# Moving pieces of a decoder kernel's seam between attention and feed-forward rows, and one normalisation inside each row

## What is computed

```
x = LN(x + attn(x))     # 16 heads of 128, decayed linear attention, silu on q k v, rms norm, sigmoid gate, Wo
x = LN(x + wkv(x, ctx)) # per channel: running sums aa, bb over the tokens, y = (e1*aa + e2*v) / (e1*bb + e2)
x = LN(x + ffn(x))      # layer norm, ternary w_fc (2048x512), exact gelu, layer norm, ternary w_proj (512x2048)
```

## Time and profile before

| | |
|---|---|
| median of 3 runs | 1342.81 us (1342.69 to 1343.02) |
| the profiled execution | 1341.81 us, of which the span of the trace is 1340.0 us |
| PE busy | 1289.2 us, 96% of the span |
| DVE, ACT, POOL busy | 964.5 us (72%), 629.8 us (47%), 297.8 us (22%) |
| chain that ended last | PE 56%, ACT 7%, issue, DVE and POOL 2% each |
| mean granted TensorE clock | 0.993 |

### The profile page before, as it was taken

The page is one execution under the profiler, slowest core; times in us unless marked ns, Lnnn a source line. Parts: engine busy times, 40 slices in busy tenths (PEclk is TensorE's granted clock), DMA queues, the critical chain, the costliest instruction groups (busy, mean ns, idle before and its releaser), DMA issues.

```text
span 1340.0 us, 20153 instructions
## 1 busy us (share of the span) xinstructions
PE 1289.2 (96%) x7468; PEld 831.7 (62%) x7468; DVE 964.5 (72%) x1882; ACT 629.8 (47%) x1138; POOL 297.8 (22%) x213
## 2 busy tenths in 40 slices
PE   5899999999999999999999999999996999999997
PEld 3566666666666666666666666666664555555553
DVE  5875775696677767766776686677778688898763
ACT  3443343334334333433443334335364678888854
POOL 2112110111011111111111111111134665555530
PEclk9999999999999999999999999999998999999999
DMA  5100021121120111011111011010010011110000
GB/s 182 63 17 16 24 88 32 48 79 64 32 71 25 48 32 40 24 57 40 36 45 32 32 48 48 17 41 16 5 59 1 33 32 48 48 48 32 17 17 32
DMA packets 19103, 55.83 MB, mean 42 GB/s; under 512 B 2624, under 2 KB 2624, under 8 KB 18624
## 3 DMA queue, kind: packets, MB, share of 16 engines
q1 hardware_dynamic: 19008, 54.55, 12.3%
HBM read 50.35 MB, written 4.19 MB: 41 GB/s over the span
## 4 chain that ended last, share of the span: by engine, by line
PE 56%; ACT 7%; issue 2%; DVE 2%; POOL 2%; POOLq 0%; ACTq 0%; DVEq 0%
PE bank L399 7%; PE bank L400 7%; PE bank L401 7%; PE bank L613 3%; PE bank L614 3%; PE bank L471 3%; PE bank L473 3%; PE bank L472 3%; PE bank L414 2%; PE bank L416 2%; PE bank L415 2%; PE bank L639 2%; PE bank L638 2%; PE bank L623 1%; PE bank L442 1%
## 5 line engine op out<-in xcount | busy, mean ns | idle before, releaser
L399 PE MATMUL bank<-x_hi,w_hi 128*128 128x512 f16 x768 | 294.2, 383 | 5.2 <-DVE w_lo L1077 2.9
L1123 DVE TENSOR_TENSOR resid<-resid,bank 128x512 f32<-128x512 f32 x256 | 173.2, 685 | 174.3 <-PE bank L473 173.7
L400 PE MATMUL bank<-x_lo,w_hi 128*128 128x512 f16 x768 | 293.2, 382 | 0.0
L401 PE MATMUL bank<-x_hi,w_lo 128*128 128x512 f16 x768 | 293.1, 382 | 0.0
L1578 POOL TENSOR_TENSOR sq_sum<-sq_sum,o_sq 128x512 f32<-128x512 f32 x64 | 106.8, 1668 | 800.5 <-ACT o_sq L757 800.5
L757 ACT ACTIVATE o_sq<-bank 128x512 f32<-128x512 f32 x64 | 38.3, 598 | 291.4 <-DVE gated L1129 291.4
L414 PE MATMUL bank<-wv_hi,x_hi 128*128 128x256 f16 x512 | 139.6, 273 | 1.0 <-DVE x_lo L1138 0.5
L415 PE MATMUL bank<-wv_lo,x_hi 128*128 128x256 f16 x512 | 139.6, 273 | 0.0
L416 PE MATMUL bank<-wv_hi,x_lo 128*128 128x256 f16 x512 | 139.6, 273 | 0.0
L399 PEld LDWEIGHTS bank<-x_hi,w_hi 128*128 128x128 f16 x768 | 76.3, 99 | 91.4 <-issue 19.1
L401 PEld LDWEIGHTS bank<-x_hi,w_lo 128*128 128x128 f16 x768 | 75.6, 98 | 92.1 <-issue 2.7
(11 more groups left out here) (174 smaller groups left out, 2657.1 us busy)
## 6 DMA issues: line engine op xcount, KB each, us to landing
w_raw<-w_ffn SPq DMA_DIRECT2D x32, 512.0 KB, 3.6
raw_a<-w_heads SPq DMA_DIRECT2D x32, 256.0 KB, 3.9
raw<-w_heads SPq DMA_DIRECT2D x15, 512.0 KB, 3.6
raw<-w_heads SPq DMA_DIRECT2D x18, 256.0 KB, 3.9
x_in<-x_rows SPq DMA_DIRECT2D x8, 512.0 KB, 4.4
out<-y_out SPq DMA_DIRECT2D x8, 512.0 KB, 2.6
resid<-x_t SPq DMA_DIRECT2D x3, 1024.0 KB, 8.1
val<-ctx_t SPq DMA_DIRECT2D x6, 512.0 KB, 3.5
```

The source lines that it names most:

```text
L399: mm(bk[:, :], a, c, start=kt == 0, stop=False)
L400: mm(bk[:, :], a, d, start=False, stop=False)
L401: last = mm(bk[:, :], b, c, start=False, stop=kt == KT - 1)
L1123: tt(resid[:, 4 * g + t, :], resid[:, 4 * g + t, :], YB[t % 2][:, :], ALU.add).then_inc(y_added, 1)
```

## The change

In the last pair, unit 6: ACT's `exps1(1, 1)` and `exps2(1, 1)` move ahead of `square(61)` and the evacuation of G. DVE's `aa_states(0)` moves ahead of `split_probs(61)`, and `correct(0, 0)`, `correct(0, 1)` ahead of `gate(61)`; `input_sum(2)` leaves the unit. Unit 7: both halves of `split_x2(0)` and DVE's `bb_states(1)` move ahead of `square(62)` and `gate(62)`; `input_norm(2)` and `shift(NX, 2)` leave the unit.

Behind the last pair: `input_sum(2)` now stands behind `add_y(62, 3)` and ahead of `gate(63)`; `scale_columns` and `shift(NX, 2)` follow `gate(63)`, and `aa_states(1)` follows the last `add_y`. On POOL `miss(0)` goes ahead of `numerator(0)`, and `root(NX, 2)` from ahead of `second_root(0)` to behind `add_squares(62)`.

In every row with an `input_norm`, now row 0 too, it stands behind the second gelu instead of ahead of the first.

```diff
@@ ACT, unit of the last pair
+                if last_pair and t == 6:
+                    exps1(1, 1)
+                    exps2(1, 1)
                 if last_pair and t == 7:
                     second_norm(0, 0, SC)
+                    split_x2(0)
                 if lag1:
                     square(u - 1)
                 evacuate(u, t, G, first_unit)
...
-                if last_pair and t == 6:
-                    exps1(1, 1)
-                    exps2(1, 1)
                 if last_pair and t == 7:
-                    split_x2(0)
-                    input_norm(2)
                     exp_ln_tables()
                     invert(1)
@@ ACT, row
-                if second_row and not first:
-                    input_norm(b + 2)
                 act.wait_ge(scfc_ok, b + 1)
                 for f in range(4):
                     gelu(b, 0, f)
                     if first and f == 1:
                         square(UNITS - 1)
+                    if second_row and f == 1:
+                        input_norm(b + 2)
@@ DVE, unit of the last pair
+                if last_pair and t == 6:
+                    aa_states(0)
                 if lag1:
                     split_probs(u - 1)
                 split_q(u)
...
-                if last_pair and t == 6:
-                    aa_states(0)
...
                 after_unit(t)
+                if last_pair and t == 6:
+                    correct(0, 0)
+                    correct(0, 1)
+                if last_pair and t == 7:
+                    bb_states(1)
+                    split_x2(0)
                 if lag1:
                     gate(u - 1)
...
-                if last_pair and t == 6:
-                    correct(0, 0)
-                    correct(0, 1)
-                    input_sum(2)
                 if last_pair and t == 7:
-                    shift(NX, 2)
                     fc_scale(0, root)
-                    bb_states(1)
-                    split_x2(0)
@@ DVE, behind the last pair
             for t in range(2, 4):
                 add_y(U - 2, GROUPS - 1, t)
+            input_sum(2)
+            gate(U - 1)
             scale_columns()
-            aa_states(1)
-            gate(U - 1)
+            shift(NX, 2)
             for t in range(4):
                 add_y(U - 1, GROUPS - 1, t)
+            aa_states(1)
             row(0, 0, first=True)
@@ POOL
+            miss(0)
             numerator(0)
-            miss(0)
...
-            root(NX, 2)
             second_root(0)
...
             add_squares(L + 6, 6)
+            root(NX, 2)
             add_squares(U - 1, 7)
```

## The result

The changed kernel takes 1334.65 us (median of five runs, 1334.36 to 1337.37) where the kernel before takes 1342.81. The ratio is 0.9946, with a 95% interval of 0.9935 to 0.9957: 5.8 to 8.7 us faster, against 7.3 forecast. The medians lie 8.2 us apart, the ratio gives 7.3. The profiled execution has a span of 1332.9 us, 7.1 under that of before.

A forecast was written before the change was run, and what follows sets the result against it. PE, busy 96% of the span, was taken as the bound, so only its idle pays, with DVE held by POOL second. Seam 5.6 plus rows 1.7 gave 7.3 us, 1342.81 to 1335.5; range 1332 to 1339, forecast chance 0.55.

The forecast's parts named there:

- turn_back(0) 5.0 us earlier: Seam, unit 7: turn_back(0) starts near 1019.2 instead of 1024.21 because mask(62) ends at 1019.1.
- The replay of DVE and POOL: Units 6 and 7: operations timed in turn, DVE's two-input ones held until POOL's running operation ends.
- a new idle of 3.6: Unit 6: PE's mix of unit 61 starts near 1009.85, not 1006.17, waiting for the held second p_lo.
- It comes from input_sum(2) leaving; the other moves nearly cancel: Seam: the 5.0 us come from input_sum(2) leaving DVE's queue before mask(62), 5.4 us; other moves cancel in holds.
- The clock gives back 1.4: Behind turn_back(0): work at 0.50 lost 0.9 us and at 0.72 lost 0.56; 1.4 comes back, bounded 0 to 1.4.
- stays at full speed: Seam: PE's clock stays full, since PE idles 3.6 and 1.8 us instead of 9.01.
- The slower rival: Seam: new idles bring PE to 1.2 GHz from 1010 over some 16 us of work, giving 1348.5; chance 0.05.
- Given back in unit 7: Unit 7 and behind: POOL holds the gate to about 1036.6, 0.6 lost; unit 63's output 6.1 or 5.1 us earlier.
- the second of my two cases: Unit 7: weighted_now(1) holds fc_scale's last operation to 1039.0; third output product near 1041.5, 3.75 us earlier.
- Rows 1.7: Rows 1 to 5: moving input_norm behind the second gelu shifts the table load by 0.35 each, 1.7 us in all.
- the step from row 6: Row 6, without input_norm: ACT idles 1.07 before the load, which stands behind the first product's wait; gap 0.51, not 0.85.
- All cover named for `turn_x1(2)` and `load_rows`: Rows: turn_x1's input is ready 1.3 us early; load_rows(b+3) is issued 3.5 us later, read over 10 us after.

The follow-up runs named there:

- e3_sum: The kernel before with only row 2's sum (input_sum(2) and what hangs on it) moved, units 6 and 7 otherwise in old order: 1341.66 us, ratio 0.9983.
- e4_aa_back: The changed kernel with aa_states(0) back behind the splits of the probabilities and of Q in unit 6: 1338.90 us, ratio 0.9970.
- e7_miss_back: The changed kernel with miss(0) back behind numerator(0) on POOL: 1336.89 us, ratio 0.9960.
- e9_fill_all: The kernel before with 40 unused matmuls on PE in the 9.01 us stall ahead of turn_back(0): 1341.08 us, ratio 0.9989.
- e5_fill: The kernel before with 32 unused matmuls on PE in the 9 us stall ahead of turn_back(0): 1343.15 us, ratio 1.0007.
- e6_preload: The changed kernel with the gelu table loaded explicitly behind invert in rows 0 to 6, ahead of the wait for the first product: 1331.19 us, ratio 0.9905.
- e10_gate_first: The changed kernel with bb_states(1) and DVE's split_x2(0) back behind gate(62) and fc_scale(0): 1335.87 us, ratio 0.9954.
- e2_seam: The changed kernel with input_norm of rows 1 to 5 back ahead of the first gelu: 1337.28 us, ratio 0.9950.
- e11_fill_gap: The changed kernel with 12 unused matmuls in the 2.83 us idle ahead of unit 62's third output product: 1334.49 us, ratio 0.9939.
- e12_best_fill: The changed kernel with gelu preload, unit 7's gate first, row 2's statistics behind the last gate, plus unused matmuls in three seam idles: 1328.70 us, ratio 0.9898.

## Why the prediction was right, and where its steps were off

- **turn_back(0) 5.0 us earlier**: measured 6.0. The replay of DVE and POOL, operation by operation with the holds, came out within 0.3 us up to the split of the probabilities (end forecast 11.6 us behind the first mask, measured 11.3) and 0.5 at the split of K; it gave the two `add_key` 0.9 too late. That is the term that was mis-sized. The mix of unit 61 was read wrong as well, without a price: it doesn't wait for both halves at once (a new idle of 3.6 forecast), but for each half alone, 0.81 and 1.68.
- **"It comes from input_sum(2) leaving; the other moves nearly cancel"**: wrong. e3_sum gives 3.8 of the 6.0. The step that failed is reading `mask(62)` as the one thing that `turn_back` waits for. It waits for the second `add_key` as well, which ended near 1020.5 (1017.21 and 3.32 us for the two), 3.6 us ahead of the end of the masks; with the masks early this became the bound. The sum's move does bring the masks 5.4 us forward (25.97 to 20.60 for their end), the number in the prediction; but `turn_back(0)` can use it only because the other moves bring the second `add_key` from 22.08 to 18.40. So the other moves don't cancel. Undoing the scans alone costs 0.6 (e4_aa_back) and undoing `miss` alone 0.9 (e7_miss_back); what `correct` ahead of the gate gives was not run alone. That the replay's total came near the measured one in spite of this is no luck, since it had all moves in it: only the attribution was wrong.
- **The clock gives back 1.4**: right in size (1.37 by e9_fill_all, and 1.35 from 5.96 at `turn_back` to 7.31 at `turn_x2` in the changed kernel). That it "stays at full speed" was right for the profiled execution and not for all. My evidence, that it fell only 5 us into an empty stretch, was one sample: e3_sum's fell within 3 us of idle, e5_fill's behind 2.1. The slower rival was right that the new idles can bring a fall, and wrong about its price: e6_preload's clock fell in the new idle of unit 61 (0.65 and 0.50 from 1010 to 1014), which cost nothing because PE waits again at `turn_back`.
- **Given back in unit 7**: the second of my two cases happened. `gate(62)` was held to 1036.5 and the last operation of `fc_scale` for 2.31 us by `weighted_now`. For this case the third output was forecast 3.75 us earlier and came 5.2 earlier, the first output of unit 63 5.1 and 6.4: one microsecond of each is that of the first point, the other 0.3 to 0.5 was not traced to a term.
- **Rows 1.7**: 1.7 measured, by the step from row 6 that the load waits for the product. All cover named for `turn_x1(2)` and `load_rows` held; no PE wait appears there.
- The sum was 7.3. At full clock it is 6.4 + 1.7 = 8.1; with one fall behind the 2.83 us it is 6.5. The runs lie in two groups, three at 1334.4 to 1334.7 and two at 1336.8 and 1337.4, and the ratio is taken over both: that it gives the forecast's 7.3 to the tenth is luck, since the seam at full clock was forecast 0.8 us too low and falls take that back.

## What to carry to other kernels

When a wait has two conditions, find the time of the second before pricing the removal of the first: the profile names only the later one. Replay a reordering on DVE and POOL together, with each two-input operation held to the end of POOL's running one; such a replay put the first output of unit 63, fifty microseconds on, within a microsecond here. And look where a table load stands relative to the wait in front of its operation: loading it in the idle before that wait gave 3.5 us of 1334.

## What the runs showed that was not expected

The clock of TensorE fell from 2.4 to 1.2 GHz behind idles as short as 1.87 us (e10_gate_first), 2.11 (e5_fill) and 2.83 (e2_seam), and not behind every such idle: behind the same 2.83 us it was 1.00 in the changed kernel and 0.58 over 4 us in e2_seam, at 1.6 us of time. The same is seen in code that no experiment touches: behind the idle of 2.1 us near 397 the clock stayed at 1.00 in four of the fourteen traces (before, e2_seam, e6_preload, e7_miss_back) and fell in the other ten, at 1.7 us of time in the changed kernel (the step between the masks at 382 and 420) and 2.9 in e5_fill. The Trainium skill (TensorE: Matmul & The Clock Gate, What's actually happening) says that the gate watches how busy PE has been in a rhythm of its own that doesn't start with the kernel, so that the same kernel varies from run to run; these traces agree, as far as traces of different kernels with the same code in these stretches can.

So a single execution, and a median of a few, can be off by 1.5 to 3 us, and positions counted from a near mark tell more than the total time. Where ten runs exist, time goes with the mean clock: in e4_aa_back from 1334.87 us at 0.994 to 1342.20 at 0.988. With unused matmuls in the seam's idles the runs lay closer together (3.0 to 1.0 us in e11_fill_gap, 3.5 to 0.8 in e12_best_fill), but on four or five runs each. Whether each single slow execution is such a fall isn't shown, since only one execution of each kernel was traced.
